# Local-attention scores of a tile in two halves, with the query projection of the next tile but one between them

## What is computed

```python
def attn_layer(x, Wqkv, qs, ksc, Wo):             # x: 1 x 2048 x 128, 16 heads of 64
    q, k, v = jnp.split(x @ Wqkv, 3, -1)          # Wqkv: 128 x 3072
    q = l2norm(q) * qs;  k = l2norm(k) * ksc      # then a rotary embedding of both
    ...
    # a window is 32 queries against their own 32 keys and the 32 before them
    sim = jnp.einsum('bhwie,bhwje->bhwij', bq, bk2) * QK_SCALE
    sim = jnp.where(mask, -jnp.finfo(sim.dtype).max, sim)
    out = jnp.einsum('bhwij,bhwje->bhwie', jax.nn.softmax(sim, -1), bv2)
    return out.reshape(b, n, INNER) @ Wo
for i in range(DEPTH):                            # DEPTH = 6
    x = attn_layer(shift_tokens(x), ...) + x
    x = ffn_layer(shift_tokens(x), ...) + x
```

## Time and profile before

| | |
|---|---|
| median of 3 runs | 2342.61 us |
| lowest and highest of them | 2341.81 and 2348.17 us |
| time of the profiled execution | 2346.82 us |
| its span, from first to last instruction | 2345.0 us |
| mean granted TensorE clock | 0.962 of full speed |
| TensorE matmul busy | 2147.4 us, 92% |
| VectorE busy | 1979.2 us, 84% |
| ScalarE busy | 1775.8 us, 76% |
| GpSimd busy | 1308.6 us, 56% |

### The profile page before, as it was taken

The page is one execution under the profiler, slowest core; times in us unless marked ns, Lnnn a source line. Parts: engine busy times, 40 slices in busy tenths (PEclk is TensorE's granted clock), DMA queues, the critical chain, the costliest instruction groups (busy, mean ns, idle before and its releaser), DMA issues. The chain is left out here.

```text
span 2345.0 us, 82133 instructions
## 1 busy us (share of the span) xinstructions
PE 2147.4 (92%) x34457; PEld 1320.3 (56%) x34457; DVE 1979.2 (84%) x2378; ACT 1775.8 (76%) x4234; POOL 1308.6 (56%) x1084
## 2 busy tenths in 40 slices
PE   5999999999996789999998999999999998999985
PEld 2122222222222677777767777777777777777763
DVE  7999999999962889888988899887888888888863
ACT  3388888888885778787787788786878887777862
POOL 4211111110102888787777788786777777777850
PEclk8699999999998999999999999999999999999987
DMA  2322232222111232433334343433343332433331
GB/s 44 93 67 81 64 84 69 79 66 62 44 67 40 63 87 74 130 99 85 93 94 114 89 110 75 126 92 86 78 126 87 93 88 73 128 81 95 83 85 32
DMA packets 167702, 194.84 MB, mean 83 GB/s; under 512 B 87398, under 2 KB 107364, under 8 KB 167332
## 3 DMA queue, kind: packets, MB, share of 16 engines
q1 hardware_dynamic: 167076, 189.59, 30.9%
q10 hardware_dynamic: 256, 0.00, 0.0%
HBM read 56.91 MB, written 25.42 MB: 35 GB/s over the span
## 5 line engine op out<-in xcount | busy, mean ns | idle before, releaser
L978 DVE TENSOR_REDUCE mx<-S_ps 128x1 f32<-128x1024 f32 x512 | 601.5, 1219 | 25.2 <-PE S_ps L1260 19.5
L725 ACT ACTIVATE PT<-E_ps 128x512 f32<-128x512 f32 x1024 | 533.6, 602 | 101.5 <-PE E_ps L1269 99.0
L641 POOL TENSOR_TENSOR tc<-tc,ts 128x1024 f32<-128x1024 f32 x192 | 463.0, 2411 | 30.0 <-DVE ts L1040 29.7
L649 POOL TENSOR_TENSOR tc<-tc,rs 128x1024 f32<-128x1024 f32 x192 | 362.5, 1909 | 13.7
L1260 PE MATMUL S_ps<-KS,QS 48*128 48x512 bf16 x1024 | 320.9, 400 | 10.3 <-DVE mx L978 4.7
L795 ACT ACTIVATE pr<-B_ps,mxB 128x64 f32<-128x64 f32 x1536 | 325.0, 371 | 0.4 <-DVE mxB L1059 0.4
L1269 PE MATMUL E_ps<-QS,KS 64*128 64x512 bf16 x1024 | 317.1, 383 | 7.4 <-ACT PT L725 5.2
L583 POOL CAST w_cut_b<-w_raw_b 128x512 fp32r<-128x512 f32 (+1 forms) x48 | 27.6, 576 | 511.7 <-DMA w_raw_b<-in_Wqkv 380.0
L603 POOL TENSOR_TENSOR pr<-pr,mxB 128x1024 f32<-128x1024 f32 x96 | 184.0, 1917 | 203.0 <-DVE mxB L1073 202.9
L1306 PE MATMUL B_ps<-w_qkv,x_cut 128*128 128x512 f32 x576 | 263.7, 458 | 24.0 <-POOL x_cut L596 9.2
L1277 PE MATMUL O_ps<-PT,va 128*32 128x512 f32 x2048 | 273.7, 606 | 0.0
(11 more groups left out here) (178 smaller groups left out, 4101.0 us busy)
## 6 DMA issues: line engine op xcount, KB each, us to landing
xy<-pc SPq DMA_DIRECT2D x768, 64.0 KB, 2.3
vs<-v SPq DMA_DIRECT2D x96, 384.0 KB, 3.7
Wqkv_cut<-w_cut_b SPq DMA_DIRECT2D x72, 256.0 KB, 2.4
w_qkv<-Wqkv_cut SPq DMA_DIRECT2D x36, 512.0 KB, 7.2
rot<-in_rot SPq DMA_DIRECT2D x96, 128.0 KB, 2.6
vs<-v SPq DMA_DIRECT2D x96, 128.0 KB, 3.7
w_raw_b<-in_Wqkv SPq DMA_DIRECT2D x36, 256.0 KB, 3.0
W_cut<-w_cut_b SPq DMA_DIRECT2D x24, 170.5 KB, 2.5
```

The source lines that it names most:

```text
L641: e.tensor_tensor(tc[:, :], tc[:, :], m.ts[i][:, :], ALU.add).then_inc(s[f"rot{n}"], 1)
L649: e.tensor_tensor(tc, tc, m.rs[u % 2][2][:, i * H:(i + 1) * H].unsqueeze(2).to_broadcast([P, H, DH]), ALU.mult).then_inc(s[f"{n}_scaled"], 1)
L725: e.activation(m.PT[n % NPT][:, :], turns.bank("probs", n)[:, :], ACT.Exp).then_inc(turns.sem("probs", n), 1)
L978: e.tensor_reduce(m.mx[h % 2][:, i, hf:hf + 1], m.S_ps[n % 2][:, :, :], AX.XY, ALU.max).then_inc(s["sc_max"], 1)
```

## The change

`score` gets a second argument. Part 0 makes all the waits, writes the mask and issues the products of the first four pairs of heads; part 1 issues those of the other four and increments `score_mm`. The step calls part 0 where it called `score`, and part 1 behind the query projection and ahead of `values`. No product is added or removed, and no wait is moved from one product to another.

```diff
-    def score(u):
+    def score(u, part):
...
-        w.wait_ge(s["qT_out0"], u + 1)
...
-        banks.wait_free(w, "score", u)
-        for par in range(2):
-            e.matmul(bank[:, par, :, :], m.ident_bf[:, :], mk, start=True, stop=False, skip_group_check=True)
-        for p in range(NP):
+        if part == 0:
+            w.wait_ge(s["qT_out0"], u + 1)
...
+            banks.wait_free(w, "score", u)
+            for par in range(2):
+                e.matmul(bank[:, par, :, :], m.ident_bf[:, :], mk, start=True, stop=False, skip_group_check=True)
+        for p in range(part * NP // 2, (part + 1) * NP // 2):
...
-        mm.then_inc(s["score_mm"], 1)
+        if part == 1:
+            mm.then_inc(s["score_mm"], 1)
...
     for u in range(FIRST, LAST):
-        score(tile(u - 3))
+        score(tile(u - 3), 0)
         finish(late(u - 12))
         project(tile(u - 1), 0)
+        score(tile(u - 3), 1)
         values(tile(u - 5))
```

More of the change, by code:

```diff
@@ L1339, in score @@
         mk = m.mask_bf[:, 0 if u % NT == 0 else 1, :, :]
-        w.wait_ge(s["qT_out0"], u + 1)
[L1341 to L1344, removed]
-        banks.wait_free(w, "score", u)
-        for par in range(2):
-            e.matmul(bank[:, par, :, :], m.ident_bf[:, :], mk, start=True, stop=False, skip_group_check=True)
-        for p in range(NP):
+        if part == 0:
+            w.wait_ge(s["qT_out0"], u + 1)
+            w.wait_ge(s["qT_out1"], u + 1)
+            w.wait_ge(s["kT_out0"], u + 1)
+            w.wait_ge(s["kT_out1"], u + 1)
+            w.wait_ge(s["mask"], 1)
+            banks.wait_free(w, "score", u)
+            for par in range(2):
+                e.matmul(bank[:, par, :, :], m.ident_bf[:, :], mk, start=True, stop=False, skip_group_check=True)
+        for p in range(part * NP // 2, (part + 1) * NP // 2):
             for par in range(2):
```

## The result

The changed kernel takes 2391.61 us (median of 4 runs, 2391.02 to 2393.84) against 2345.39 us of the kernel before, timed beside it. The ratio is 1.0187 with a 95% interval of 1.016 to 1.0214, 46 us slower. Forecast were 2409 us, 2358 to 2450.

The account below looks back on a forecast made before the run. TensorE, busy for 189.35 of 200 us in the middle of part B, was taken as the bound. Pauses 50 + borders 13 + clock 12 - 8 given back = 67 us, a median of 2409 us, range 2358 to 2450.

Parts of the forecast that it names:

- 140 places of 256: TensorE: block ends in the projection or first 128 second-half score instructions each pause 1.45 us; 50 us more, bounds 25 to 70.
- the pauses at L1371: Sign in the value products: waits by "issue" of about 100 us instead of 45.9; prediction wrong if they stay near 46.
- Borders: TensorE: an added border between large and small products costs 0.14 us a step, 13 us over 95 steps, bounds 0 and 35.
- The clock: TensorE: more time at 1.2 GHz after the added pauses, 12 us more, bounds 0 and 37.
- Given back: TensorE's waits for ACT's copies at L1347 and L1306, 18.8 us, shrink as TensorE comes later; 8 us counted.
- Borders alone: Rival on TensorE: blocks do not pause more, only borders are paid; 0 to 35 us, about 13 more, 2356 us; chance 0.09.
- DVE takes over: Rival on DVE: the slip of maxima is not covered, adding 57 us to the 67; 2466 us; chance 0.04.
- Faster: Rival: fewer pauses in the scores and shorter waits for ACT; likely 15 us less, at most 29; 2328 us; chance 0.05.

Follow-up runs that it names:

- split 2/6: Changed kernel with two pairs of heads ahead of the query projection and six behind, instead of four and four; 2435.29 us, ratio 1.038 to the kernel before.
- mask first: Changed kernel with only the mask written ahead of the query projection and all eight pairs of heads behind it; 2510.87 us, ratio 1.07 to the kernel before.
- split 6/2: Changed kernel with six pairs of heads ahead of the query projection and two behind, instead of four and four; 2346.5 us, ratio 0.9994 to the kernel before.
- 5/3 split: Changed kernel with five pairs of heads ahead of the query projection and three behind, instead of four and four; 2366.18 us, ratio 1.0079 to the kernel before.
- 7/1: Changed kernel with seven pairs of heads ahead of the query projection and one behind, instead of four and four; 2364.41 us, ratio 1.0082 to the kernel before.
- late-signal kernel: Kernel before, in its old order, but score_mm incremented by the fifth query projection matmul instead of the last score product; 2348.74 us, ratio 1.0017.
- kernel with the scores around half of the projection: Changed kernel with the second half of the scores between the projection's first three and other three matmuls; 2368.66 us, ratio 1.0073 to the kernel before.

## Why the prediction was right, and where not

**Pauses: the mechanism right, the size four to five times too large.** The step that failed is the first term, "140 places of 256": it forecast 50 us more of pauses, and 11 were measured. It let the next block be asked for when the array reaches the end of the block in use. The traces read better if it is asked for when TensorE's queue takes in the last instruction of the block, ahead of what the array runs. How far ahead the queue is can be read from its own semaphore waits. In the changed kernel the last one ahead of the values is taken in 0.22 or 0.23 us before the first value product in 74 of 95 steps, some 40 small instructions; in the kernel before, where the projection stands there, it is 1.7 us in 22 steps and less in most others. If the block ends early in the second half of the scores, the queue reaches that end before or during the projection, and the block comes while the six matmuls run. Two steps of the changed kernel show it. In the first the block in use ended at about 1198.84, 0.53 us into the second half; in the second at about 1288.98, right at its beginning.

```profile
1198.31 0.86 PE L1353 MATMUL B_ps<-k_T,q_T 64*32 64x64 f32 x64
...
1202.41 0.19 PE L1371 MATMUL B_ps<-xy,vs 64*64 64x32 f32 x1 [1.36 <-issue]
...
1288.94 0.86 PE L1353 MATMUL B_ps<-k_T,q_T 64*32 64x64 f32 x64
```

The windows of the two (columns as in the earlier trace rows):

```profile
1198.84:1202.42 3.58, 2.22 (x151) 2.01 (x141) 3.55 (x5) 0.85 (x1) 3.26 (x5) 1.00 0.35 77
1288.98:1290.77 1.79, 1.79 (x137) 1.70 (x136) 1.53 (x2) 1.45 (x4) 1.79 (x2) 1.00 0.01 5
```

In the first, a block's worth of instructions took 3.58 us, with the pause in it, about what a block costs to bring. In the second, as many ran in 1.79 us without a pause. (The counts in brackets take in what was already under way at the edges.)

To see it for all steps I numbered the instructions on TensorE's queue in the trace (each load twice, for its matmul, and each wait for a semaphore), with a block end every 256 as the pauses give them, and summed the gap at the following block end by the place of this one, counted from the step's first load. The second half of the scores spans places 145 to 274 in the changed kernel, the projection 262 to 274 in the kernel before. Gaps in us, in brackets how many are over 1.1 us, of how many:

```
place of block end   0-128       128-192     192-256     256-276
before            28.4 (6/45)  10.6 (2/25)  19.2 (8/26)  12.1 (7/7)
changed           18.8 (6/45)   7.1 (2/25)  46.1 (25/26) 10.4 (6/7)
split 2/6         23.0 (6/45)  42.8 (24/25) 45.2 (25/26) 10.7 (6/7)
mask first        62.0 (25/45) 43.8 (24/25) 47.6 (25/26) 13.5 (6/7)
split 6/2         20.9 (6/45)  10.1 (1/25)  18.8 (7/26)  13.0 (7/7)
```

Past the first 50 instructions of the second half nearly every block end is followed by a pause, of 1.8 us on average; before them almost none. That makes about 80 bad places, not 140, and some 20 of these (256 to 276) were bad before as well, with some of the others. What is new is 27 us there, and 15 us less at the other places together. The 5/3 split fits: its second part begins at place 177, and all 13 block ends from place 230 to 255 are followed by a gap of 1.0 us or more, 4 of the same 13 before.

Two things the run-ahead alone doesn't explain: the last column of the kernel before, where seven of seven ends pause although the block could have been asked for with the projection still to run, and the pauses of 7/1. It may be that the block in use had itself come late there; no run shows it.

The page Runtime: NRT & Kernel Launch of the Trainium skill, section Instruction fetch mechanics, gives TensorE room for 2048 instructions and calls block crossings mostly hidden. Here they were not wherever the code was dense: 38 pauses of over 1.1 us in the scores and values of the changed kernel, 79 with the mask first, all at block ends, and the measurement decides. Where and how long a block takes was read rightly in the prediction: by the count of instructions the block of the earlier trace rows begins at 1007.76 us (1007.8 there) and ends at 1011.52. Of its own signs the pauses at L1371 came to 62.5 us, not about 100, but didn't stay near 46 either.

**Borders.** 0.16 us a step in the median, 15 us in 95 steps; 13 were forecast.

**The clock.** 35 us more at 1.2 GHz between 800 and 2250 us cost up to 17 us; 12 were forecast. This holds as far as the matmuls in such stretches run at half speed, as those at 1420.05 do. Over the whole span it is 51 us more (232 against 181), up to 25 us; but the late-signal kernel, as fast as the kernel before, has 205 us. So a single trace gives this term to 10 us at best.

**Given back.** I counted 8 us of ACT's waits as given back. Corrected for the missing records these did not fall (20 us, from 18.8). All waits of TensorE on others together, so corrected, went from 51 to 45 us between 800 and 2300 us, although the one for the layer's weights at L1306 rose from 0.8 to 4.6: so 6 us came back, from other waits than I had named.

**The sum.** 11 + 15 + 17 - 6 = 37 us, or 45 with the clock of the whole span, against 46 measured (44 between the two profiled executions); 67 were forecast. Direction and mechanism were right. That the total came out as near as it did was partly luck: the pauses, 39 us less than forecast, lie below the low end of their own bounds (25 to 70), and borders and clock made part of it good by coming out larger.

**The rivals.** "Borders alone" falls with the series of splits. In the changed kernel they are 15 of the 46 us, and in the kernel with the scores around half of the projection about the whole loss, so they are no small thing. "DVE takes over" falls with the late signal and with 6/2, which cost nothing though DVE waits for the scores in both. "Faster" had one part right, the pauses in the scores went from 6.6 to 0.8 us.

## What to carry to other kernels

Where a kernel has hundreds of tiny instructions in a row on one engine, count instructions as well as time: bringing 256 of them takes about 3.5 us here, and code that runs 256 in 2 us mostly pauses where it crosses a block end without slower work close ahead. Dense code wants to be parted by long instructions, and two dense runs shouldn't be joined; but each border between small and large products cost 0.07 to 0.2 us here. A pause of 1.5 us can also cost afterwards, through TensorE's clock, as it did behind about half of them in the changed kernel. And before a grown wait is explained, compare the number of records with the number of instructions.

## What the runs showed of the hardware

The block ends could be found to the instruction: in the changed kernel the gaps in scores and values of over 1.1 us all fit a step of 256. I had not expected that a dense stretch of 320 instructions would cost the same as one of 256 (0.9994), and one of 448 3.8% more. Nor that a kernel with 37 of 46 us of these pauses gone would still be 35 us slower: the matmuls that were moved to hide the blocks were missed where they had hidden ACT's copy. 45 us of the loss are in the three waits named there; the rest is not taken apart.
